# A two-layer attention and feed-forward kernel: 244 of the 1024 softmax denominators are summed by VectorE instead of ScalarE, and the order of the steps is laid out again

## The reference, cut to what matters

```python
x = x + attn(layernorm(x)); x = x + ffn(layernorm(x))
# attn:
qkv = x @ Wqkv                        # 16 heads of 16
q_rot, k_rot = rotate(q), rotate(k)   # cos and sin tables
num = exp(q_rot @ k_rot.T * scale)
den = sum(exp(q @ k.T * scale), axis=-1)      # plain q and k, all 1024 keys
y = where(causal, num / den, 0) @ v ;  y @ Wout + bout
# ffn:
out_shared = relu(x @ Ws1) ** 2 @ Ws2
prob = trunc(softmax weights of the top 2 of 8 logits)   # nonzero only where a weight is 1
out = out_shared + sum_e prob_e * (relu(x @ W1_e) ** 2 @ W2_e)
```

## Time and profile before

| | before |
|---|---|
| median of 3 runs | 1653.8 us (1652.38 to 1654.6) |
| the profiled execution, own time | 1653.4 us |
| its span in the trace | 1651.7 us |
| ScalarE busy | 1592.1 us (96%) |
| TensorE busy | 1502.0 us (91%) |
| VectorE busy | 845.9 us (51%) |
| GpSimd busy | 531.2 us (32%) |
| first and last exponential of a score tile | start at 34.33, end at 1625.25 us |

### The profile page before, as it was taken

The page is one execution under the profiler, slowest core; times in us unless marked ns, Lnnn a source line. Parts: engine busy times, 40 slices in busy tenths (PEclk is TensorE's granted clock), DMA queues, the critical chain, the costliest instruction groups (busy, mean ns, idle before and its releaser), DMA issues.

```text
span 1651.7 us, 25986 instructions
## 1 busy us (share of the span) xinstructions
PE 1502.0 (91%) x8442; PEld 598.3 (36%) x8442; DVE 845.9 (51%) x1949; ACT 1592.1 (96%) x2651; POOL 531.2 (32%) x919
## 2 busy tenths in 40 slices
PE   8888989999999989999899899999999999999988
PEld 6322333333333333333333333333333333333325
DVE  5334434765346653566445554566534765445515
ACT  2999999999999999999999999999999999999994
POOL 3324133432234322343333323334133432234310
PEclk9998999999999999999999999999999999999998
DMA  5432233331434313343234333343243331433300
GB/s 165 152 100 80 86 106 116 116 105 55 132 115 131 115 36 125 116 131 106 77 112 123 104 96 116 106 122 97 83 132 115 117 105 54 131 115 106 116 26 27
DMA packets 95391, 172.09 MB, mean 104 GB/s; under 512 B 15696, under 2 KB 82256, under 8 KB 83152
## 3 DMA queue, kind: packets, MB, share of 16 engines
q1 hardware_dynamic: 94656, 169.55, 33.0%
q10 hardware_dynamic: 592, 0.79, 0.1%
HBM read 111.55 MB, written 58.72 MB: 103 GB/s over the span
## 4 chain that ended last, share of the span: by engine, by line
ACT 87%; PE 7%; issue 3%; DVE 1%; POOL 0%; DVEq 0%; DMA 0%; POOLq 0%; ACTq 0%
ACT scores L546 57%; ACT probs L556 27%; ACT probs L558 4%; PE scores L622 2%; PE y_ps L651 1%; PE side L661 1%; PE scores L629 1%; PE side L603 1%; PE side L680 0%; PE scores L809 0%; POOL v_sb L424 0%; PE scores L814 0%; DVEq L927 0%; DMA qk_parts<-parts 0%; PE scores L804 0%
## 5 line engine op out<-in xcount | busy, mean ns | idle before, releaser
L546 ACT ACTIVATE scores<-scores 128x1024 f32<-128x1024 f32 x1024 | 1067.1, 1119 | 16.4 <-PE scores L622 16.1
L622 PE MATMUL scores<-stack 96*128 96x512 bf16 x2048 | 583.5, 384 | 67.3 <-ACT scores L546 39.2
L556 ACT ACTIVATE probs<-scores 128x1024 f32<-128x1024 f32 x512 | 491.9, 1109 | 3.7 <-PE scores L629 2.6
L629 PE MATMUL scores<-stack 96*128 96x512 bf16 (+3 forms) x1536 | 335.6, 330 | 47.0 <-ACT scores L546 38.0
L443 POOL TENSOR_SCALAR_AFFINE_SELECT probs<-probs 128x256 f32<-128x256 f32 (+1 forms) x640 | 241.9, 406 | 380.5 <-ACT probs L556 220.1
L651 PE MATMUL y_ps<-probs,v_sb 128*32 128x512 f32 (+3 forms) x3072 | 331.8, 504 | 5.2 <-POOL probs L443 5.1
L622 PEld LDWEIGHTS scores<-stack 96*128 96x128 bf16 x2048 | 152.6, 97 | 473.6 <-ACT scores L546 207.7
L546 ACT ACTIVATION_READ_ACCUMULATOR scores<-scores 128x1 f32 x1024 | 297.6, 291 | 0.0
L453 POOL TENSOR_TENSOR parts<-rest,parts 128x512 bf16<-128x512 f32 x124 | 143.4, 1156 | 293.1 <-DVE parts L994 293.1
L629 PEld LDWEIGHTS scores<-stack 96*128 96x128 bf16 x1536 | 117.0, 98 | 300.6 <-ACT scores L546 154.6
L451 POOL TENSOR_TENSOR rot<-raw,cos_sb 128x512 f32<-128x512 f32 x62 | 89.4, 1442 | 389.1 <-DVEq L1004 389.1
(11 more groups left out here) (140 smaller groups left out, 1116.9 us busy)
## 6 DMA issues: line engine op xcount, KB each, us to landing
stack<-qk_parts SPq DMA_DIRECT2D x756, 128.0 KB, 2.6
qk_parts<-parts SPq DMA_DIRECT2D x127, 384.0 KB, 2.6
out<-x_mid SPq DMA_DIRECT2D x32, 256.0 KB, 2.9
x_in<-in_L_attn_x SPq DMA_DIRECT2D x7, 1024.0 KB, 5.3
stack<-qk_parts SPq DMA_DIRECT2D x18, 64.0 KB, 2.3
x_in<-in_L_attn_x SPq DMA_DIRECT2D x2, 512.0 KB, 4.5
probs<-in_L_attn_Wqkv SPq DMA_DIRECT2D x1, 512.0 KB, 5.8
cos_sb<-in_cos SPq DMA_DIRECT2D x1, 512.0 KB, 6.5
```

Source lines behind the costliest of these rows:

```text
L546: nc.scalar.activation(src, src, ACT.Exp, scale=SCALE, accum_out=den[:, g % 2, i, j:j + 1]).then_inc(exp_done, 1)
L556: nc.scalar.activation(probs[:, chunk % 2, j, :], src, ACT.Exp, scale=SCALE).then_inc(exp_done, 1)
L622: mm = nc.tensor.matmul(tile[:, half * HALF:(half + 1) * HALF], q[:, j, i * P:(i + 1) * P], k[:, j, half * HALF:(half + 1) * HALF], start= ...
L629: mm = nc.tensor.matmul(tile[:, col:col + n], k[:, h, i * P:(i + 1) * P], q[:, h, q0:q0 + n], start=True, stop=True)
```

## The change

It does seven things.

1. For 244 den steps, chosen in `SUMMED` (10, 4, 6 and 12 in units 0 to 3, 6 in the last unit, 4 in the first), ScalarE's exponential goes without an accumulator output into one of two new SBUF tiles `sum_tiles`, and VectorE sums it: `sum_den`, three steps later in VectorE's order (`SUM_LAG`), one scalar_tensor_tensor that adds the two halves of 512 columns and gives the sum as accumulator output. ScalarE waits, before it writes a sum tile, for the sum of two before (`summed`).
2. The product of the plain q/k with the cosines moves from GpSimd to VectorE, which reads it from PSUM; `raw` is gone, the copy goes to `rest`, and the shuffle moves from the "turn" tile to the plain one.
3. `ORDER`, `PV_STEPS`, `SIDE`, `TAKE_Y`, `RECIPROCALS`, `STATS1`, `STATS2`, `COPY` and `GAP` have new values.
4. In the first batch TensorE runs four idle matmuls (`keep_busy(4)`) at each of the steps whose side tile doesn't exist there.
5. At the end the up products of the pair 0 and 1 come before the second half of the logits, `exp_gap` goes behind ScalarE's last tiles, and the routed count behind the last down product.
6. A few buffers share space (`hidden`, `logits_t`, `gate`, `w1_now`, `w2_now`), and `ones` is one column wide.
7. The reciprocals have one more drain of VectorE ahead of them.

```diff
-ORDER = [5, (0,), 4, (1,), 3, (2,), 7, (3,), 6, (4,), 7]
+ORDER = [5, (0,), 4, (1,), 5, (2,), 6, (3,), 5, (4,), 7]
-ORDER_FIRST = [16, (0,), 1, (1,), 1, (2,), 1, (3,), 1, (4,), 12]
-ORDER_LAST = [0, (0,), 4, (1,), 0, (2,), 7, (3,), 11, (4,), 10]
+ORDER_FIRST = [14, (0,), 0, (1,), 1, (2,), 5, (3,), 4, (4,), 8]
+ORDER_LAST = [2, (0,), 3, (1,), 0, (2,), 4, (3,), 16, (4,), 7]
+SUM_SLOTS, SUM_LAG = 2, 3
+SUMMED = [
+    (3, 6, 8, 10, 13, 18, 19, 23, 26, 28),
+    (10, 20, 21, 25),
+    (2, 7, 13, 18, 23, 27),
+    (0, 3, 6, 8, 9, 12, 13, 15, 23, 24, 26, 27),
+    (2, 11, 13, 18, 25, 26),
+    (4, 12, 15, 17),
+]
...
@@ low_part (GpSimd)
-                if t % 2 == 0:
-                    pool.wait_ge(raw_ready, at(b, 8, 2 * g + t // 2 + 1))
-                    nc.gpsimd.tensor_tensor(rot[:, :], raw[:, :], cos_sb[:, t // 2 * HALF:(t // 2 + 1) * HALF], ALU.mult)
@@ act_step (ScalarE)
+                    if s in SUM_AT[unit_of(b, g)]:
+                        k = sums_ahead(b, g) + SUM_AT[unit_of(b, g)][s]
+                        if k >= SUM_SLOTS:
+                            act.wait_ge(summed, k - SUM_SLOTS + 1)
+                        nc.scalar.activation(sum_tiles[:, k % SUM_SLOTS, :], src, ACT.Exp, scale=SCALE).then_inc(exp_done, 1)
+                        return
@@ side_step (TensorE)
+                if first and kind not in ("end", "turn") and not runs(kind, g, first, last):
+                    for k0, b0, n0 in before:
+                        pe.wait_ge(taken[k0], (at1 if k0 in ("ffn", "gen") else at)(b0, TILES[k0], n0 + 1))
+                    keep_busy(4)
+                    return before
@@ qk_tile (VectorE)
-                    nc.vector.tensor_copy(raw[:, :], side).then_inc(taken["qk"], 1)
-                    dve.drain().then_inc(raw_ready, 1)
-                    split(0, raw[:, :])
+                    nc.vector.tensor_copy(rest[:, :], side)
+                    nc.vector.tensor_tensor(rot[:, :], side, cos_sb[:, cols], ALU.mult).then_inc(taken["qk"], 1)
+                    settle()
+                    nc.vector.tensor_copy(parts[:, 0, 0, :], rest[:, :])
+                    nc.vector.stream_shuffle(turned[:, :], rest[:, :], PARTNER)
+                    settle()
+                    nc.vector.tensor_tensor(rest[:, :], rest[:, :], parts[:, 0, 0, :], ALU.subtract)
                     middle(0)
                 else:
-                    nc.vector.stream_shuffle(turned[:, :], raw[:, :], PARTNER)
-                    settle()
+            def sum_den(b, g, s):
+                _, j, i = STEPS[unit_of(b, g)][s]
+                tile = sum_tiles[:, (sums_ahead(b, g) + SUM_AT[unit_of(b, g)][s]) % SUM_SLOTS, :]
+                dve.wait_ge(exp_done, at(b, G * NSTEP, g * NSTEP + s + 1))
+                nc.vector.scalar_tensor_tensor(tile[:, 0:HALF], tile[:, 0:HALF], 0.0, tile[:, HALF:C], ALU.add, ALU.add,
+                                               accum_out=den[:, g % 2, i, j:j + 1]).then_inc(summed, 1)
@@ END_TILES
-             ... ("t2", 0), ("t2", 1), ("logits", 0), ("up", 0), ("up", 1), ("down", 0), ("routed", 0), ("down", 1)]
+             ... ("t2", 0), ("t2", 1), ("up", 0), ("up", 1), ("logits", 0), ("down", 0), ("down", 1), ("routed", 0)]
```

More of the change, by code:

```diff
@@ L90, in unit_of, with summed_steps, sums_ahead @@
     return G if b == B - 1 and g == G - 1 else G + 1 if b == 0 and g == 0 else g
+SUM_SLOTS, SUM_LAG = 2, 3
[7 more added lines that the diff above has]
+]
+def summed_steps(steps, chosen):
+    dens = [s for s, x in enumerate(steps) if x[0] == "den"]
+    return {dens[d]: k for k, d in enumerate(chosen)}
+SUM_AT = [summed_steps(steps, chosen) for steps, chosen in zip(STEPS, SUMMED)]
+def sums_ahead(b, g):
+    return sum(len(SUM_AT[unit_of(n // G, n % G)]) for n in range(b * G + g))
 PIECES = [(0, 0), (0, 1), (1, 0), (1, 1), (2, 0), (2, 1), (2, 2), (3, 1), (3, 0), (3, 2), (4, 0), (4, 1)]
 PV_STEPS = [
[6 rows of a table removed]
[6 rows of a table added]
 ]
@@ L104 @@
 Y_FIRST, Y_LAST = [(0, 0), (3, 0)], [(3, 1), (4, 1)]
-TAKE_Y = [47, 42, 37, 42, 36, 39]
+TAKE_Y = [41, 41, 39, 46, 32, 37]
 LOW_LAG = 3
-RECIPROCALS = (32, 25, 16, 25)
+RECIPROCALS = (24, 36, 17, 15)
 SIDE = [
[L117 to L129, removed]
@@ new lines @@
+    {0: ("qk", 0), 4: ("v", 0), 8: ("v", 1), 13: ("v", 2), 19: ("turn", 1), 21: ("qk", 2), 26: ("turn", 3),
+     27: ("v", 3), 36: ("norm", 0), 39: ("norm", 1), 47: ("acc", 0)},
+    {0: ("qk", 0), 6: ("turn", 1), 9: ("qk", 2), 16: ("acc", 1), 18: ("acc", 2), 20: ("turn", 3),
+     22: ("acc", 3), 31: ("t2", 0), 33: ("t2", 1), 36: ("t2", 2), 38: ("t2", 3), 40: ("route", 0),
+     46: ("route", 1), 49: ("ffn", 0)},
+    {1: ("qk", 0), 5: ("ffn", 1), 10: ("route", 2), 12: ("turn", 1), 13: ("qk", 2), 17: ("ffn", 2),
+     23: ("norm", 0), 25: ("norm", 1), 26: ("turn", 3), 30: ("acc", 0), 33: ("acc", 1), 37: ("acc", 2),
+     42: ("ffn", 3), 47: ("xt", 0)},
@@ L130 @@
+    {0: ("xt", 1), 2: ("xt", 2), 4: ("xt", 3), 5: ("acc", 3), 8: ("qk", 0), 14: ("ffn", 4), 17: ("ffn", 5),
+     21: ("turn", 1), 23: ("qk", 2), 28: ("turn", 3), 34: ("ffn", 6), 37: ("ffn", 7)},
+    {2: ("acc", 3), 5: ("ffn", 4), 10: ("ffn", 5), 14: ("ffn", 6), 17: ("ffn", 7), 35: ("end", 0),
+     37: ("end", 1), 38: ("end", 2), 45: ("end", 3), 48: ("end", 4)},
+    {2: ("qk", 0), 6: ("v", 0), 9: ("turn", 1), 11: ("v", 1), 16: ("qk", 2), 22: ("v", 2), 24: ("turn", 3),
+     26: ("v", 3)},
 ]
@@ L217, in block @@
         xn2t = sb("xn2t", [P, KC, C])
-        hidden = sb("hidden", [P, 2 * P])
+        hidden = turned[:, 0:2 * P]
         hidden2 = sb("hidden2", [P, 2, 2 * P])
-        logits_t = sb("logits_t", [P, 2 * P])
+        logits_t = turned[:, 0:2 * P]
         logits = sb("logits", [P, NB, E])
@@ L257, in block @@
         chunk_used = sem("chunk_used")
+        summed = sem("summed")
         y_ready = sem("y_ready")
@@ L721, in route_tile @@
                     pe.wait_ge(weight_ready, at(b, 1, 1))
-                    mm = nc.tensor.matmul(side[:, 0:NB], ones[:, :], weight[:, :], start=True, stop=True)
+                    mm = nc.tensor.matmul(side[0:1, 0:NB], ones[:, :], weight[:, :], start=True, stop=True)
                 mm.then_inc(full["route"], 1)
@@ L1136, in end_tile @@
                     spread_reciprocals((t,))
-                if tile == ("down", 0):
+                if tile == ("down", 1):
                     route(b)
```

38 lines of the change are left out of this document (21 added, 17 removed), and 12 rows, old and new, of the table PV_STEPS.

## The result

The changed kernel takes **1666.4 us** (median; 1666.04 to 1670.48) against 1653.8 us (1652.38 to 1654.6): the ratio is 1.0085, with a 95% interval of 1.0073 to 1.0097. The change makes the kernel 0.85% slower. The forecast was 1624 us, in the range of 1616 to 1637, and "faster" with 0.91.

What follows compares the result with a forecast made beforehand. ScalarE's list of exponentials was taken as the bound, busy 96% of the span. The sum was 1653.4 - 30.5 + 3 - 2.5 + 0.7 - 0.5 = 1623.6 us, stated as 1624, range 1616 to 1637 us.

Steps and rivals of the forecast that it cites:

- the change part by part: The prediction's section that priced each part of the change in turn, engine by engine, then the first batch and the tail.
- the added tile in unit 0: TensorE: the first out-projection tile, about 0.9 us, makes unit 0 47.3 of 48.2 us; it still fits.
- GpSimd loses 62 x 1.44 us; its masks can only come sooner: GpSimd: its load falls by that much, to about 440 us busy, and nothing of its work comes later.
- the waits that the new tables bring: ScalarE's waits for TensorE in seven batches, with shorter units and bursts of side work: 3 us added, bounds 0 and 12.
- Rival A: TensorE becomes the bound in and around unit 0: 1638 us, chance 0.18; sign: den and num product waits over 15 us.
- The saving: ScalarE: 244 den steps without accumulator output cost 0.905 instead of 1.03 us, so 30.5 us leave the path.
- The sums' deadlines: VectorE's sums at 1.2 us each (bounds 0.70 and 1.75) are never late for ScalarE: 0 us.
- Rival B: VectorE's sums come late and ScalarE waits for them, slower than before: 1685 us, chance 0.06.
- VectorE's load: VectorE busy time goes from 846 to about 1122 us, 69% of the new span, and stays off the path.
- The first batch: Start of the kernel: spread num steps and idle matmuls give -2.5 us; a first num step awaiting the gather, +0.7 us.
- The end: Tail behind the last exponential: the new order of products and routed count gives -0.5 us, bounds -2 and +1.

Runs made afterwards that it cites:

- experiment 1: The changed kernel with GpSimd's copy put back from step 28 to step 43 of unit 1: 1639.3 us, ratio to before 0.9923.
- experiment 4: The kernel before with only GpSimd's copy moved from step 43 to step 28 of unit 1: 1692.0 us, ratio 1.0224.
- experiment 6: The changed kernel with the copy at step 43 and the first out-projection tile back at step 3 of unit 1: 1625.3 us, ratio 0.9823.
- experiment 7: The changed kernel with the copy at step 43 and two idle matmuls at each of steps 3 to 8 of unit 1: 1626.5 us, ratio 0.984.
- experiment 9: The version of experiment 6 with an empty choice of sums: 1647.1 us, ratio to before 0.9966.
- experiment 3: The changed kernel with an empty choice of sums, all denominators by ScalarE's accumulator: 1669.0 us, ratio to before 1.0092.
- experiment 5: The changed kernel with the copy at step 43 and an empty choice of sums: 1656.4 us, ratio to before 1.0015.
- experiment 2: The changed kernel with the tables of the kernel before, except the first taking of y at step 43: 1693.1 us, ratio 1.0231.
- experiment 11: The version of experiment 6 without the four idle matmuls at the first batch's missing side tiles: 1628.4 us, ratio to before 0.9852.

## Why the prediction was wrong

The step that failed is in "the change part by part": the new values of the tables. I costed two of them from their place in the order of time (the first unit and the added tile in unit 0), and the others not at all. "GpSimd loses 62 x 1.44 us; its masks can only come sooner" passes over the copy, which moved by 15 steps. In the sum the waits that the new tables bring stand as 3 us, with 12 as the upper bound; two entries of the tables alone brought 27.1 and 14.0.

**The copy.** It costs 27 us (experiment 1, and 38.6 us alone in experiment 4). The price was in a row of my own: a VectorE instruction of 0.70 us took 1.60 beside a GpSimd instruction with two inputs. I used it for the sums, where it did little (median 0.685 us), and not for the chain of small operations that the copy was moved next to, on which TensorE waits. Nor did I ask what TensorE's clock does behind such a wait: it falls to half, in all seven batches.

**TensorE in unit 1.** I weighed only whether the work fits the unit, and found the place to be feared in unit 0, which got the tile. The harm lay in unit 1, which gave it: too little work in one place. It costs 14 us (experiments 6 and 7). Rival A has the right engine and the wrong reason. The sign that I had named for it, waits for the score products of over 15 us, showed with 48.3 us, though its work wasn't too much for any unit. Its price of 1638 us was too low, and it lay outside my own range, which ended at 1637.

**The saving.** The price of a step held to the last digit (medians of 1.03 and 0.905 us in batch 3 of experiment 6). The term of 30.5 us was too large all the same, since it takes ScalarE to be the bound at every step: 23.6 to 23.9 us came out (experiment 9). Even with the two causes gone, the saving is 6.6 us short of its term.

**The sums' deadlines.** Right for the new tables: no wait of ScalarE for VectorE. The sum takes 0.69 + 0.08 us where I took 1.2. The rule of half throughput in the Trainium skill (Vector Engine (DVE) Microarchitecture Reference, section Points that are easy to get wrong) doesn't describe this instruction here: with two fp32 sources in SBUF and an accumulator output its median for 512 columns is 685 ns, the mean of a tensor_tensor of the same size in the kernel before 702. What I missed is that a sum that is in time for ScalarE can still be in the way of VectorE's next work: one sum of 0.77 us stands ahead of the layernorm chain, and the copy costs 27.1 us with the sums and 12.6 without them (experiments 3 and 5). Rival B exists, under the old tables (experiment 2).

**VectorE's load.** 1009.6 us busy for a forecast of 1122; with 0.77 us a sum the same working gives 846 - 17 + 188 = 1017. GpSimd is busy 476.4 us for a forecast of 440: the third parts take 1.40 us each where they took 1.16.

**The first batch.** The first num step started at 50.5 us, where I had 50.8. ScalarE's wait for it was still 2.35 us and not 0.7, since ScalarE was ready at 48.2 and not at 50.1: the first exponential began 0.9 us sooner, and waits ahead of it were gone. Behind it TensorE's clock is at half from 51 to 53 us. The granted clock of unit 1 was 0.97, not the 0.90 of before. What the idle matmuls are worth is open between 0.6 and 3 us (experiment 11).

**The end.** 4.4 us shorter for a forecast of 0.5: the order gives 2.2; another 2.2 go together with the clock that held.

The account of the stretch: 1590.9 - 30.5 + 27.1 (copy) + 14.0 (clock in unit 1) + 7.4 (first unit and small waits, the rest) = 1608.9 us. With the two causes removed, the kernel takes 1625.3 us, 1.3 us from the forecast. That closeness is in part luck: the saving was 6.6 us too large in my sum, and the end 3.9 us too small.

## What to carry to other kernels

When a change comes with new tables, go through every moved item, on every queue, and ask what it now runs beside; an item of GpSimd with two SBUF inputs must not lie beside a chain of small VectorE operations that another engine waits for. When an engine is near its bound and its clock depends on what it does, a gap is as dangerous as a crowd: look for stretches that lose work, not only for those that gain it. And test a table by putting back one entry at a time; two entries of some 150 made the difference between 0.85% slower and 1.8% faster.

## What the runs showed of the hardware

A VectorE operation on 8 columns takes 0.17 us alone and 0.60 to 0.63 us while GpSimd runs additions of two SBUF tiles of 256 columns (0.69 us each), whatever its kind: tensor_tensor, scalar_tensor_tensor, and in experiment 4 also operations with one tensor input (0.50 to 0.62 us). The pace, 0.68 us from start to start, is that of GpSimd's instructions, and it ends with the last of them. I read this so: a small operation isn't done before the GpSimd instruction that it meets, whatever its own bytes.

TensorE's granted clock fell to half behind a stretch of 4 us in which it was busy 62% of the time, and behind standstills of some 3 to 4 us: behind ScalarE's wait of 2.97 us in experiment 2 came 2.4 us more of waits at the lower clock. The busy share alone doesn't foretell it. In experiment 3 a stretch of 4 us with the same 62% (2.49 us) was followed by the full clock:

```profile
919.00:923.00 4.00, 2.49 (x20) 0.54 (x20) 3.70 (x7) 4.00 (x9) 4.00 (x7) 1.00 0.52 172
923.00:930.00 7.00, 6.66 (x44) 3.54 (x44) 5.37 (x12) 6.04 (x9) 3.28 (x9) 1.00 0.68 200
```

Adding idle matmuls in the gap of unit 1 held the clock there and made the kernel 12.8 us faster (experiment 7).
